# Slot mixture: running maximum from the logits' banks, logits and turned shares in pairs, last pair behind the first slots

## The reference

```
logits   = einsum('bmd,dnp->bmnp', x, phi)                    # x is the normalised row
dispatch = softmax(logits, axis=0)                            # over the batch: per position and slot
combine  = softmax(logits.reshape(b, m, n * p), axis=-1)      # over all slots: per token
slots    = einsum('bmd,bmnp->bnpd', x, dispatch)
y        = einsum('bnpd,nde->bnpe', slots, W) + b[None, :, None, :]
out      = einsum('bnpd,bmnp->bmd', y, combine)
```

## Time and profile before

| | us |
|---|---|
| median of 3 runs | 1069.25 |
| lowest, highest | 1068.12, 1069.73 |
| the profiled execution, time | 1070.25 |
| the profiled execution, span | 1068.5 |
| TensorE matmuls, busy | 860.7 (81%) |
| VectorE, busy | 791.5 (74%) |
| ScalarE, busy | 570.3 (53%) |
| POOL, busy | 445.7 (42%) |

### The profile page before, as it was taken

The page is one execution under the profiler, slowest core; times in us unless marked ns, Lnnn a source line. Parts: engine busy times, 40 slices in busy tenths (PEclk is TensorE's granted clock), DMA queues, the critical chain, the costliest instruction groups (busy, mean ns, idle before and its releaser), DMA issues. The chain is left out here.

```text
span 1068.5 us, 26400 instructions
## 1 busy us (share of the span) xinstructions
PE 860.7 (81%) x10387; PEld 623.1 (58%) x10387; DVE 791.5 (74%) x1840; ACT 570.3 (53%) x1300; POOL 445.7 (42%) x286
## 2 busy tenths in 40 slices
PE   4173498789839995789879898989898988878888
PEld 3062354678626764445556676767676766644567
DVE  4989787678665544788787859586877768788964
ACT  4172144467614444467687464655647483346764
POOL 4101020597226775298206333342516262618710
PEclk9597699899859998699979999999999999999989
DMA  5411000400061114000100000000000100000001
GB/s 155 114 53 79 1 1 0 164 3 2 6 226 45 53 51 101 12 1 2 28 23 2 26 4 26 2 26 3 26 20 9 27 2 2 3 1 2 2 2 40
DMA packets 27127, 35.95 MB, mean 34 GB/s; under 512 B 7835, under 2 KB 20444, under 8 KB 26238
## 3 DMA queue, kind: packets, MB, share of 16 engines
q1 hardware_dynamic: 21310, 27.84, 8.2%
q0 software_dynamic: 2496, 5.12, 1.7%
q10 hardware_dynamic: 3200, 1.31, 0.5%
HBM read 26.98 MB, written 7.27 MB: 32 GB/s over the span
## 5 line engine op out<-in xcount | busy, mean ns | idle before, releaser
L1829 PE MATMUL soft_expert_ps<-soft_W,soft_slots 128*32 128x128 f32 x4096 | 136.9, 276 | 15.7 <-issue 8.6
L2100 DVE TENSOR_TENSOR soft_outs<-soft_expert_ps,soft_bias 128x512 f32<-128x512 f32 x128 | 87.0, 686 | 73.4 <-PE soft_expert_ps L1829 73.4
L1829 PEld LDWEIGHTS soft_expert_ps<-soft_W,soft_slots 128*32 128x32 f32 x4096 | 105.2, 110 | 47.7 <-issue 43.2
L1921 ACT ACTIVATE soft_slots<-soft_slot_ps 128x512 f32<-128x512 f32 x128 | 69.3, 593 | 78.2 <-PE soft_slot_ps L1815 76.4
L945 POOL TENSOR_TENSOR l_prob<-l_prob,l_inv 128x1024 f32<-128x1024 f32 x48 | 91.3, 1901 | 42.2 <-DVE l_inv L1099 41.6
L2002 POOL TENSOR_TENSOR l_ring<-l_ring,soft_inv 128x1024 f32<-128x1024 f32 x15 | 39.1, 2632 | 106.2 <-DVE soft_inv L2093 57.7
L1084 DVE TENSOR_REDUCE l_under<-l_score 128x16 f32<-128x1024 f32 x48 | 58.7, 1222 | 29.0 <-PE l_score L1162 14.8
L2002 POOL TENSOR_TENSOR soft_spread<-soft_spread,soft_inv 128x1024 f32<-128x1024 f32 x16 | 41.3, 2610 | 73.9 <-DVE soft_inv L2093 73.9
L974 PE MATMUL l_turned<-ident,l_prob 128*128 128x128 f32 x384 | 53.3, 283 | 22.5 <-POOL l_prob L945 22.5
L1843 PE MATMUL soft_mix_ps<-soft_outs,soft_combT 128*64 128x128 f32 x1024 | 70.1, 279 | 1.5 <-DVE soft_acc L2116 1.5
L1048 ACT ACTIVATE l_probT<-l_turned 128x512 f32<-128x512 f32 x96 | 52.2, 594 | 34.8 <-PE l_turned L974 34.8
(11 more groups left out here) (435 smaller groups left out, 2196.4 us busy)
## 6 DMA issues: line engine op xcount, KB each, us to landing
moe_w<-in_moe_W SPq DMA_DIRECT2D x2, 2048.0 KB, 10.2
soft_W<-in_soft_W SPq DMA_DIRECT2D x16, 256.0 KB, 2.7
kept<-early SPq DMA_DIRECT2D x1, 2048.0 KB, 6.3
l_keys<-in_moe_b SPq DMA_DIRECT2D x1, 2048.0 KB, 8.6
l_asked<-kept SPq DMA_DIRECT2D x1, 2048.0 KB, 13.2
ctxT<-in_ctxT SPq DMA_DIRECT2D x1, 1024.0 KB, 5.2
moe_rows<-xn_tok SPq DMA_DIRECT2D x4, 256.0 KB, 3.7
expert_rings<-moe_back SPq DMA_DIRECT2D x4, 256.0 KB, 5.8
```

What stands on the lines that cost most here:

```text
L1829: last = nc.tensor.matmul(expert_ps[c][32 * j:32 * j + 32, h, tt, :], slots[u % 3][:, h, tt, 128 * c + 32 * j:128 * c + 32 * j + 32], W[i ...
L1921: last = nc.scalar.activation(slots[u % 3][:, h], slot_ps[h][:], ACT.Copy)
L2100: nc.vector.tensor_tensor(outs[u % 3][:, c].rearrange("p h t d -> p (h t) d"), expert_ps[c][:].rearrange("p h t d -> p (h t) d"), bias[i % ...
```

## The change

For j of 2 and up, the running maximum reads the logits from the bank `slot_ps[k % 2]` instead of the copy in SBUF, and comes ahead of the reduction of the same k. VectorE still waits for `logit_taken` first. So that a bank is not written over before it has been read, `logits(j, k)` for k of 3 and up also waits for the maximum step of k - 2, and `fill_slots(i, 0)` for the last one. For j of 0 and 1 the maximum reads the copy as before and comes after the reduction.

Between two groups, TensorE and ScalarE take logits k + 2 of group i + 1 and turn k of group i in turns, for k of 0 to 6, and turn 7 comes behind `fill_slots(i, 0)` on TensorE and behind `take_slots(i, 0)` on ScalarE. In group 0, turn 7 moves in the same way, with no logits between the turns.

```
             def logits(j, k):
                 if k >= 2:
                     pe.wait_ge(logit_taken, 8 * j + k - 1)
+                    if j >= 2 and k >= 3:
+                        pe.wait_ge(high_step, 7 * j + k - 2)
...
                 else:
                     pe.wait_ge(logit_taken, min(8 * i + 16, 8 * I))
+                    if 1 <= i < I - 1:
+                        pe.wait_ge(high_step, 7 * i + 14)
...
             turn(0, 0)
             turn(0, 1)
             swap_part(0)
-            for k in range(2, 8):
+            for k in range(2, 7):
                 turn(0, k)
...
                 if i:
                     mix(i - 1, 7)
-                    if ahead:
-                        for k in range(2, 8):
-                            logits(i + 1, k)
-                    for k in range(8):
+                    for k in range(7):
+                        if ahead and k + 2 < 8:
+                            logits(i + 1, k + 2)
                         turn(i, k)
                 fill_slots(i, 0)
+                turn(i, 7)
...
                 if i and ahead:
-                    for k in range(8):
-                        take_logits(i + 1, k)
-                for k in range(8):
+                    take_logits(i + 1, 0)
+                    take_logits(i + 1, 1)
+                for k in range(7):
+                    if i and ahead and k + 2 < 8:
+                        take_logits(i + 1, k + 2)
                     take_turned(i, k)
                 for g in range(8):
                     take_slots(i, g)
+                    if g == 0:
+                        take_turned(i, 7)
...
-            def survey(j, k):
-                dve.wait_ge(logit_taken, 8 * j + k + 1)
-                here = spread[j % 2][:, 2 * k:2 * k + 2, :]
-                nc.vector.tensor_reduce(own[:, j, 2 * k:2 * k + 2], here, AX.X, ALU.max, negate=True).then_inc(own_done, 1)
+            def heighten(j, k, own):
                 if k == 1:
                     if j:
                         dve.wait_ge(tall_done, j)
-                    nc.vector.tensor_tensor(high[:], spread[j % 2][:, 0:2, :], here, ALU.max).then_inc(high_step, 1)
+                    nc.vector.tensor_tensor(high[:], spread[j % 2][:, 0:2, :], own, ALU.max).then_inc(high_step, 1)
                 elif k:
                     dve.wait_ge(high_step, 7 * j + k - 1)
-                    nc.vector.tensor_tensor(high[:], high[:], here, ALU.max).then_inc(high_step, 1)
+                    nc.vector.tensor_tensor(high[:], high[:], own, ALU.max).then_inc(high_step, 1)
+
+            def survey(j, k):
+
+                here = spread[j % 2][:, 2 * k:2 * k + 2, :]
+                dve.wait_ge(logit_taken, 8 * j + k + 1)
+                if j >= 2:
+                    heighten(j, k, slot_ps[k % 2][:])
+                nc.vector.tensor_reduce(own[:, j, 2 * k:2 * k + 2], here, AX.X, ALU.max, negate=True).then_inc(own_done, 1)
+                if j < 2:
+                    heighten(j, k, here)
```

## The result

| | before | after |
|---|---|---|
| median of 4 runs, us | 1068.68 | 1053.98 |
| lowest to highest | 1065.95 to 1069.73 | 1052.08 to 1054.18 |
| ratio, 95% interval | | 0.9858 (0.9842 to 0.9874) |
| span of the profiled execution | 1068.5 | 1052.2 |
| VectorE busy | 791.5 | 758.2 |

The kernel is 14.7 us faster; 15.0 were forecast (1054.3). The median of the kernel before is here over one execution more than in the table ahead of the prediction (1069.25). TensorE does the same work; VectorE has lost 33 us of being held up.

The account below looks back on a forecast made before the run. TensorE's stalls between a group's last mix and the next second `experts` step were taken as the bound. Six groups at 2.5 us give 15.0, taking the profiled 1070.25 to 1055.3, the median to 1054.3 us; range 1050 to 1061.

Parts of the forecast that it names:

- What bounds: TensorE's stalls between a group's last mix and the next second `experts` step; TensorE full in the even part.
- The price of a maximum from PSUM: Seven VectorE maximum steps per group reading PSUM: 0.67 us each if free, 2.25 if held up.
- the fast end: Maximum from PSUM as fast as a free step: 0.67 us, start to start 0.60.
- The pairs: Logits and turns alternating between groups: 1.7 us of gaps go; stalls 0.55 ahead of logits 4, 0.8 ahead of first slots.
- Turn 7: Behind the first slots it costs TensorE nothing, lying in the 1.23 us wait for the slots' copies.
- Where it counts: 2.5 us in each of groups 1 to 6, 15.0 in sum; 0 in groups 0 and 7.
- A: Rival, slower: POOL holds up the maximum steps in spite of their PSUM operand; +17, so 1086 us; chance 5%.
- B: Rival: VectorE faster, but bank loop or waits inside pairs eat the order's gain; 1.6 us a group, 1059.6; chance 13%.
- C: Rival, nothing: the even part comes late by as much, or VectorE is not freed; 1069 us; chance 3%.

Follow-up runs that it names:

- reduction-first kernel: The kernel after, with each survey's reduction ahead of its maximum again for all j: 1079.78 us, ratio 0.9918 to the kernel before.
- order-only kernel: The kernel before with the new order on TensorE and ScalarE, maximum from the copy, no new waits: 1077.64 us, ratio 1.0071 to before.
- turn-7 kernel: The kernel after with turn 7 back ahead of the first slots in all groups: 1054.50 us, ratio 0.9864 to before.
- last from copy: The kernel after with each group's seventh maximum reading the SBUF copy: ratio 0.9769 to before; again, 1046.74 us against 1052.66 for the kernel after.

## Why the prediction was right, and where it was off

**What bounds.** Right: the even part stayed full (27.50 of 27.50 us busy from 664.3 to 691.8), and what the front lost came out of the time one for one.

**The price of a maximum from PSUM.** I took the fast end, 0.67 to 0.69 us; measured 0.687. What spoke against it, 0.065 us more for a PSUM source, an estimate from figures of the Trainium skill ("VectorE: DVE Perf Modes", section on the trn2 errata), is not borne out: 0.687 against a free 0.677 us from SBUF, and 0.60 from start to start in both.

**The pairs.** Right in kind, 0.26 us too long up to the first slots. I had charged 0.55 us ahead of logits 4; the gap was 0.3, as maximum 2 ended 3.91 us behind the mix and not 4.03, and logits 4 started 0.15 us behind it and not 0.2. A free pair took 1.30 and not 1.35 us, which gave only 0.02 in all, as the first pair behind a wait took 1.37. The stall ahead of the slots, charged 0.8, was 0.7. These terms were mis-sized, in one direction. Taking 2.5 where the dates gave 2.6 added 0.1. Measured: 2.84 us in each of groups 2, 4, 5 and 6 within 0.02.

**Turn 7.** I said that it costs nothing and fills the 1.23 us; so it does, but it had another effect that I did not state: it spares 0.3 us ahead of the slots, as the kernel with turn 7 ahead shows.

**Where it counts.** Six groups: right, with 3.0 on the mean, as the swap of group 1 had waited 1.39 us and group 3 got back 0.9 us of slow clock, which I had left to the range. Group 0: right, nothing. Group 7: the step that failed. "Turn 7 moves beneath that wait: 0" is true of the work, since the wait ends at the same distance from mix(6, 7), but it grew from 2.80 to 3.31 us, and behind it the clock stood at a mean of 0.56 for 6.8 us. That took back 2.3 us. That the forecast's 15.0 came out so near the measured 14.7 is in part luck: 18.1 in the groups, less 2.3 in group 7, with 0.5 from parts that the change does not touch, make the 16.3 us between the two spans, and the profiled execution before was 1.6 us above its median (1070.25 against 1068.68), that after at its own. Two terms were each off by 2 to 3 us, and the sum by 0.3.

**The rivals.** A, which the kernel with the copy as operand brings about, gave 52.66 us a group and 1086.6 us where I had worked out 1086; its condition, a held-up operation, was false for the real change. B did not come about: the loop over the banks did fit, by a margin that the reduction-first kernel shows to be under 0.6 us. (Its price was added up slightly wrong, six times 1.6 us being 9.6 and not 9.7; nothing hangs on it.) C fell with the even part. What the forecast did not say is that each half of the change alone would land at C or worse.

## What to carry to other kernels

When VectorE's two-operand steps take two or three times their usual time, look for POOL beside them; one operand left in PSUM, or a place in the order where POOL has nothing to do, takes the whole hold-up away, and small operations suffer as much as large ones (2.3 us for 16 columns, 2.25 for 512). A relieved engine and a better order can each be worth nothing alone and several us together: follow the next wait in both before judging either. Where a bank is handed on through several engines, put the reader that releases it first; work that no one waits for comes behind.

## What the runs showed of the hardware that I had not expected

The granted clock fell to 1.2 GHz behind a wait of TensorE of 3.5 to 3.7 us in each of the groups 1 to 6 of the order-only kernel (mean 0.70 over 8 us in group 2) and behind one of 3.3 us in group 7 of the kernel after (0.56 over 6.8 us). But the same 2.80 us of waiting in group 7 were followed by a clock of 1.00 in the kernel before and by 1.2 GHz in the turn-7 kernel (mean 0.64 over 4.7 us), and two profiles with 3.32 us (kernel after, last from copy) differ by 1.2 us in what followed, a difference that a second profile of each repeats. What else decides is open.

The profile's releaser is the event that came last, not the one waited for: at five of the six first slots it named POOL's product. The kernel in which that product ended 0.6 us after the slots' start shows that the slots did not wait for it.
